# Experts' down product as six matmuls on high and low halves, with the down weights split tile by tile on ScalarE and GpSimd

## The reference

```python
x = hidden_states.reshape(-1, hidden_dim)              # 4096 x 512, after a layernorm
routing_weights = sigmoid(x @ Wg.T)                    # 8 experts
_, top_k_index = lax.top_k(routing_weights + bias, 2)  # 2 experts a token
expert_w = ...                                         # their weights, over their sum
h1 = einsum('th,efh->tef', x, W1)
h3 = einsum('th,efh->tef', x, W3)
g = silu(h1) * h3 * expert_w[:, :, None]
out = einsum('tef,ehf->th', g, W2)                     # the down product; FFN = 256
```

## Time and profile before

| | us |
|---|---|
| median of 3 runs | 2990.41 (2989.74 to 2998.49) |
| the profiled execution's own time | 2994.48 |
| its span | 2993.0 |
| busy in the span: TensorE / VectorE / ScalarE / GpSimd | 2650.0 / 1905.4 / 1376.0 / 1000.0 |
| granted TensorE clock, mean | 0.957 |

### The profile page before, as it was taken

One profiled execution on the slowest core, in us unless ns is written; L12 is line 12 of the kernel. 1 busy time (PEld: TensorE's weight loads), 2 busy tenths in 40 slices (PEclk: granted clock), 3 DMA queues, 4 the chain that ended last, 5 costly groups with the idle time before them and its releaser, 6 DMA issues. The chain is left out here.

```text
span 2993.0 us, 49729 instructions
## 1 busy us (share of the span) xinstructions
PE 2650.0 (89%) x15042; PEld 1820.6 (61%) x15043; DVE 1905.4 (64%) x3930; ACT 1376.0 (46%) x2757; POOL 1000.0 (33%) x1210
## 2 busy tenths in 40 slices
PE   7999999999999999997688888888888734589998
PEld 6888888888888888885233333333333222356665
DVE  6555566556556665555788888888888557344443
ACT  4333444444334443333376667677766632222222
POOL 2111122211112221113355556555654447122222
PEclk9999999999999999998799999999999867799999
DMA  3110011122101111102767677767666456545554
GB/s 113 43 42 15 28 42 42 42 68 87 43 3 40 42 42 42 42 29 56 131 118 127 129 137 133 135 126 139 127 127 120 83 187 242 170 78 99 99 99 83
DMA packets 141060, 265.55 MB, mean 89 GB/s; under 512 B 39216, under 2 KB 42160, under 8 KB 139456
## 3 DMA queue, kind: packets, MB, share of 16 engines
q1 hardware_dynamic: 114064, 200.83, 29.2%
q0 software_dynamic: 23856, 58.61, 10.1%
q10 hardware_dynamic: 3072, 5.25, 0.5%
HBM read 139.43 MB, written 64.90 MB: 68 GB/s over the span
## 5 line engine op out<-in xcount | busy, mean ns | idle before, releaser
L1420 DVE TENSOR_REDUCE b_negmax<-b_ps_s 128x2 f32<-128x1024 f32 x512 | 615.8, 1221 | 113.6 <-PE b_ps_s L1563 108.3
L1292 ACT ACTIVATE b_probs<-b_ps_s 128x1024 f32<-128x1024 f32 x512 | 517.2, 1022 | 262.4 <-PE b_ps_s L1574 261.1
L260 POOL TENSOR_SCALAR probs<-probs,rinv 128x256 f32<-128x256 f32 x256 | 242.6, 947 | 1099.6 <-DVE rinv L412 1099.6
L294 ACT ACTIVATE probs<-ps_s,negmax 128x128 f32<-128x128 f32 x256 | 94.2, 368 | 481.7 <-DVE negmax L405 481.7
L1574 PEld LDWEIGHTS b_ps_s<-b_stack 56*128 56x128 f32 x1024 | 96.8, 186 | 336.7 <-issue 182.3
L1574 PE MATMUL b_ps_s<-b_stack 56*128 56x512 f32 x1024 | 252.2, 491 | 55.2 <-DVE b_negmax L1420 38.5
L1563 PE MATMUL b_ps_s<-b_stack 54*128 54x512 f32 x1024 | 228.0, 442 | 80.5 <-ACT b_probs L1292 50.2
L1585 PE MATMUL b_ps_o<-b_probs,b_v_stack 128*32 128x512 f32 x2048 | 281.3, 622 | 5.7 <-ACT b_probs L1292 5.7
L516 PE MATMUL ps_proj<-xT_h,wq_h 128*128 128x512 f32 x512 | 215.6, 421 | 0.0
L2231 POOL DMA_INDIRECT out<-e_y,e_place_int x71 | 110.6, 1558 | 313.3 <-DMA out<-e_y,e_place_int 171.2
L516 PE MATMUL ps_proj<-xT_h,wq_l 128*128 128x512 f32 x512 | 201.3, 393 | 0.0
(11 more groups left out here) (315 smaller groups left out, 6793.0 us busy)
## 6 DMA issues: line engine op xcount, KB each, us to landing
b_stack<-b_split SPq DMA_DIRECT2D x240, 128.0 KB
e_row<-rows_by_expert SPq DMA_DIRECT2D x71, 258.0 KB
x_in<-in_x SPq DMA_DIRECT2D x16, 1024.0 KB, 7.6
b_out_tiles<-row_sum_inverses SPq DMA_DIRECT2D x64, 256.0 KB
x<-acc SPq DMA_DIRECT2D x15, 1024.0 KB, 5.0
b_stack<-b_late SPq DMA_DIRECT2D x96, 128.0 KB
acc<-in_x SPq DMA_DIRECT2D x8, 1024.0 KB, 6.0
acc<-x SPq DMA_DIRECT2D x8, 1024.0 KB, 5.9
```

The source lines that it names most:

```text
L260: nc.gpsimd.tensor_scalar(probs[:, s, P:3 * P], probs[:, s, P:3 * P], rinv[:, s, 1:2], None, ALU.mult).then_inc(probs_done, 1)
L294: nc.scalar.activation(probs[:, s, 0:P], ps_s[s][:, 0:P], ACT.Exp, bias=negmax[:, s, 0:1], accum_out=rowsum[:, s, 0:1])
L1292: nc.scalar.activation(probs[:, k % 2, p, :, :], ps[:], ACT.Exp, scale=0.25).then_inc(e_done, 1)
L1420: nc.vector.tensor_reduce(negmax[:, k, p, :], ps[:], AX.X, ALU.max, negate=True).then_inc(m_reduced, 1)
```

## The change

The down product takes the form of the other one: `g` transposed and the down weights are each split into a high and a low part in fp32r, and three matmuls are made for each of the two blocks of depth, six in all, in place of two in fp32.

- TensorE: `down` waits for `gT_low` and `w2_low` and makes 6 matmuls of 128x512.
- ScalarE: `gT_copy` writes the high part of `gT` and also waits for `y_filled`; after `high(u+1)` a new step, `down_weights_high(u)`, waits, loads the expert's number and copies that expert's `w2` (128x1024) to `w2_of[i][0]`.
- VectorE: a new step `g_low(u-1)` stands at the head of the tile, ahead of `low(u+1)`.
- GpSimd: a new step `down_weights_low(u)` stands at the head of the tile, ahead of the add of tile u-1: it waits for `w2_high`, loads the expert's number and subtracts, 128x1024, two inputs in SBUF.

```diff
-        gT = sb("gT", [P, FT, P])
+        gT = [sb(f"gT_{s}", [P, FT, P], F32R) for s in "hl"]
+        w2_of = [[sb(f"w2_{s}{i}", [P, FT, H], F32R) for s in "hl"] for i in range(2)]
...
+        def expert_at(eng, u):
+            at = tile_expert_int[0:1, u:u + 1] if isinstance(u, int) else tile_expert_int[0:1, bass.ds(u, 1)]
+            return bass.ds(eng.value_load(at, min_val=0, max_val=E - 1), 1)
...
+                def down_weights_low(u, i):
+                    pool.wait_ge(w2_high, u + 1)
+                    if not isinstance(u, int) or u >= 2:
+                        pool.wait_ge(y_filled, u - 1)
+                    nc.gpsimd.tensor_tensor(w2_of[i][1][:], w2[:, expert_at(pool, u), :, :].rearrange("p o f h -> p (o f) h"),
+                                      w2_of[i][0][:].bitcast(F32), ALU.subtract).then_inc(w2_low, 1)
+
                 def tile(u, t, i):
+                    down_weights_low(u, i)
                     if not isinstance(u, int) or u:
                         add_to_tokens(u - 1, 1 - i)
...
                 def gT_copy(u):
                     act.wait_ge(g_transposed, u + 1)
-                    nc.scalar.activation(gT[:], ps_g[:], ACT.Copy).then_inc(gT_done, 1)
+                    if not isinstance(u, int) or u:
+                        act.wait_ge(y_filled, u)
+                    nc.scalar.activation(gT[0][:], ps_g[:], ACT.Copy).then_inc(gT_high, 1)
+
+                def down_weights_high(u, i):
+                    if isinstance(u, int) and u == 0:
+                        act.wait_ge(w2_loaded, 16)
+                    if not isinstance(u, int) or u >= 2:
+                        act.wait_ge(y_filled, u - 1)
+                        wait_alone(act, w2_low, u - 1, (gT_high, 1))
+                    nc.scalar.activation(w2_of[i][0][:], w2[:, expert_at(act, u), :, :].rearrange("p o f h -> p (o f) h"),
+                                         ACT.Copy).then_inc(w2_high, 1)
...
+                def g_low(u):
+                    dve.wait_ge(gT_high, u + 1)
+                    nc.vector.tensor_tensor(gT[1][:], ps_g[:], gT[0][:].bitcast(F32), ALU.subtract).then_inc(gT_low, 1)
...
                 def tile(u, t, i):
+                    if not isinstance(u, int) or u:
+                        g_low(u - 1)
                     if not isinstance(u, int) or u < TILES - 1:
                         low(u + 1, 1 - i)
...
-                def down(u, i, e):
-                    pe.wait_ge(gT_done, u + 1)
-                    if isinstance(u, int) and u == 0:
-                        pe.wait_ge(w2_loaded, 16)
+                def down(u, i):
+                    pe.wait_ge(gT_low, u + 1)
+                    pe.wait_ge(w2_low, u + 1)
                     if not isinstance(u, int) or u >= 2:
                         pe.wait_ge(y_copied, u)
+                    n = 0
                     for f in range(FT):
-                        w = w2[:, e, f, :] if isinstance(e, int) else w2[:, bass.ds(e, 1), f, :].rearrange("p o h -> p (o h)")
-                        ins = nc.tensor.matmul(ps_y[i][:], gT[:, f, :], w, start=(f == 0), stop=(f == FT - 1))
+                        for a, c in PASSES:
+                            ins = nc.tensor.matmul(ps_y[i][:], gT[a][:, f, :], w2_of[i][c][:, f, :],
+                                                   start=(n == 0), stop=(n == 3 * FT - 1))
+                            n += 1
                     ins.then_inc(y_filled, 1)
```

More of the change, by code:

```diff
@@ L2201, in run_experts @@
         g_transposed = sem("g_transposed")
-        gT_done = sem("gT_done")
+        gT_high = sem("gT_high")
+        gT_low = sem("gT_low")
+        w2_high = sem("w2_high")
+        w2_low = sem("w2_low")
         w13_loaded = [sem(f"w13_loaded{n}") for n in range(2)]
@@ L2259, in tile @@
                         high(u + 1, 1 - i)
+                    down_weights_high(u, i)
                     act.wait_ge(h_filled, u + 1)
@@ L2334, in _ @@
                 in_steps(dve, TILES, tile, first=E, last=3)
+                g_low(TILES - 1)
                 y_copy(TILES - 1, (TILES - 1) // 2, (TILES - 1) % 2)
@@ L2376, in tile @@
                     e = expert_of(i)
-                    e_before = None if first else expert_of(1 - i)
                     if isinstance(u, int) and SPLIT_FIRST <= u < E:
@@ L2389, in tile @@
                                 if not first:
-                                    down(u - 1, 1 - i, e_before)
+                                    down(u - 1, 1 - i)
                                 if not last:
@@ L2402, in _ @@
                 g_transposes(TILES - 1)
-                down(TILES - 1, (TILES - 1) % 2, expert_of((TILES - 1) % 2))
+                down(TILES - 1, (TILES - 1) % 2)
 def decoder_layer(nc, x, context, mask, mask_cols, a_wq, a_wkv, a_wd, x_wq, x_bq, x_wk, x_bk, x_wv, x_bv,
```

## The result

Four runs of the changed kernel gave a median of 3038.05 us (3031.24 to 3046.59), the kernel before beside them 2990.07 us: a ratio of 1.0159, interval 1.0140 to 1.0178, which is slower by 47.5 us. I had forecast 3012 us and a range up to 3037, so the result lies outside the range. The sign and the main mechanism came as forecast; the size is more than twice the +21 us of the sum.

A forecast was written before the change was run, and what follows sets the result against it. TensorE sets the pace, the row-load loop through `meta` nearly as tight. Steady tiles +14.4, splitting tiles +3.8, first tile +1, landings +2, end 0: together +21 us on 2990.4, 3012 us; 8-in-10 range 2982 to 3037.

The forecast's parts named there:

- `meta` held to the subtraction's end: VectorE: `e_is_best`, sharing a port lock with GpSimd's subtraction, ends at +5.45 and `meta` at +5.97, 1.2 us later than now.
- the row loop as the bound: Late `meta`, 1.03 us on SyncE, then a row load of 3.95 us, needed two tiles later: a tile of 5.48 us.
- `down` behind `g_low` as the second: TensorE: `g_low` queues behind `meta` and ends near +6.5, `down` is due at +6.06: a tile of 5.15 us at least.
- the first tiles' copy: First tile: ScalarE's 1.05 us copy of the down weights stands ahead of the first gate, +1 us.
- clean gain: Rival, chance 0.15: `meta` isn't held up because the subtraction starts after it; 2971 to 2981 us.
- even: Rival, chance 0.14: `meta` is late but rows land in some 3.3 us, `down` sets 5.15 to 5.25 us; 2990 to 2998 us.
- the row load in full company: Rival, chance 0.21: loads still take 4.7 us, or ScalarE's register load isn't hidden; 3026 to 3041 us.
- when GpSimd subtracts: GpSimd: after ScalarE's copy ends at +2.28 and a 0.71 us register load, the subtraction runs from +3.05 to +5.41.
- one mean load in one bound: Row load taken as 3.95 us, from 2.9 to 4.7, giving a tile of 5.48 us that covers the wait at `down`.
- the landings at +2: GpSimd: adds that wait for landings also hold back the subtraction behind them, about eight times 0 to 0.7 us, +2 us.
- the splitting tiles: Six tiles at the start: `e_is_best` ends at 2613.7 instead of 2613.08, delaying `c_w_l` by 0.6 us each, +3.8 us.
- the end: Last adds: the landings of adds set the time as now, 0 us.

The follow-up runs named there:

- e6_meta_before: The kernel before with VectorE's meta(u+1) moved ahead of low(u+1) and the old down product kept: ratio to before 0.9971.
- e5_combo: The changed kernel with meta(u+1) ahead of low(u+1), register loads ahead of the waits, and GpSimd's subtraction behind the add in tiles 0 to 3: 0.9938 of before.
- e3_loads: The changed kernel with the register loads of the expert's number on ScalarE and GpSimd put ahead of their waits: ratio to before 1.0076.
- e8_noadds: The changed kernel with each add to out replaced by a DMA of 128 numbers within SBUF: one execution, 5.39 us a steady tile.
- e12_combo8: The changed kernel with meta(u+1) ahead of low(u+1), register loads ahead of waits, and the subtraction behind the add in tiles 0 to 7: 0.9950 of before.
- e9_swap_first8: The changed kernel with GpSimd's subtraction behind the add, meant for the first eight tiles but effective in tiles 0 to 3 only: ratio to before 1.0121.
- e2_meta: The changed kernel with VectorE's meta(u+1) moved from behind g(u) to between g_low(u-1) and low(u+1): ratio to before 0.9970.
- e7_lock_meta: The kernel before plus an unread GpSimd subtraction ahead of each add, with meta(u+1) ahead of low(u+1): ratio to before 1.0058.
- e10_memset: The kernel before plus a GpSimd fill of a 128x2048 spare buffer ahead of each add: one execution, 5.21 us a steady tile.
- e1_nosplit: The changed kernel with the down weights split for tiles 0 and 1 only, later tiles reusing those: ratio to before 0.9973.

## Where the prediction was right, and which steps failed

**Right.** The sign, and the way of the loss. The down product: 1.71 to 1.40 us said, 0.31 less; with the rows out of the way the median tile takes 5.22 us with the old product (e6_meta_before) and 4.88 with the new (e5_combo), 0.34 less. `meta` held to the subtraction's end; the row loop as the bound; `down` behind `g_low` as the second; no wait for the split weights; the clock at 1.00 in the steady stretch; the first tiles' copy, +1 us (12.2 instead of 11.1 us for the first two). The sign to look for was not quite met: I had said `e_is_best` of 1.5 us and more in nearly every tile, and it is so in 28 of 58. In others `e_not_best` or `e_best_weight` is the one that is held; one of the three takes 1.5 us or more in 42 tiles.

The rivals "clean gain" and "even" are out. The number fell into "the row load in full company", 3026 to 3041 us, though its condition held for part of the tiles only: tiles 10 to 25 had loads of 4.3 us and more, but the mean load was 3.71 us, not 4.7, and ScalarE's register load was hidden.

**The step that failed, first: "when GpSimd subtracts".** I had the subtraction at +3.05 and its end at +5.41; medians are +3.64 and +6.02. The copy starts at +1.47 and not at +1.23 (I had put nothing between the end of `high` and the copy; it is 0.2 us), and from the copy's end to the subtraction it is 1.11 us instead of 0.77. By e3_loads the register load is 0.86 of that, where I had 0.71, and 0.25 remain without it, where I had 0.06. The row load is issued at +7.50 on average instead of +7.00. Half of that a tile, 60 times, is +15 us.

**Second: one mean load in one bound.** The load's mean, 3.71 us, was even below my 3.95, worth -7 us. But I put the mean into the rows' bound and let the other bound, which I had at 5.15 us, lie below it throughout. The loads come in groups of tiles. In tiles 10 to 25 every one took 4.3 to 5.3 us, and a tile 6.02 us on average. In tiles 26 to 33 every one took 2.6 to 3.4 us, and a tile still 5.45: the rows land early, but `down` waits for `g_low`, so these tiles don't win back what the others lost. One of them:

```profile
2790.74 2.36 DVE L2327 TENSOR_TENSOR e_not_best<-e_row,c_tile_expert 128x1 f32<-128x1 f32 x1
...
2793.47 0.42 DVE L2319 TENSOR_TENSOR e_gT_l<-e_ps_g,e_gT_h 128x256 fp32r<-128x256 f32 x1
```

```profile
2791.79 0.60 PE L2378 MATMUL e_ps_x<-c_ident,e_row 128*128 128x128 f32 x4
...
2793.94 0.50 PE L2395 MATMUL e_ps_y<-e_w_h,e_gT_h 128*128 128x512 f32 x1 [0.85 <-DVE e_gT_l L2319]
```

`down` starts at +2.15 instead of +1.13, although the rows had landed 0.5 us before their transposes. On average rows lay there for 0.28 us; half of that, 60 times, is +8 us. 15 - 7 + 8 = 16 us, which takes the 14.4 of the sum to +30.5. (Exact to a tenth is luck: I also had the old tile at 5.24 us and it is 5.27, -2 us, and the landings at +2.) That both bounds act is shown by e8_noadds (5.39 us with the rows never late).

**Third: the splitting tiles, +0.6 us each.** They cost +1.6. The mechanism was named, but the row was the wrong one: in the earlier trace rows `e_is_best` began at 2612.93, +5.1 in its tile; that tile's transposes began with TensorE still at 1.2 GHz (granted clock 0.50 from 2607.80 to 2609.90, behind the wait of 3.87 us that ended at 2603.80). In the five other tiles it began at +4.1 to +4.6, so there the subtraction's end, +5.4 by my own sum, puts it off by 0.7 to 1.2 us and not by 0.6. In the changed kernel `c_w_l` starts 1.3 us later on average (+6.3 instead of +5.0), and TensorE waits for it 32.7 us in all instead of 23.2:

```profile
PE e_ps_h L2393 <- DVE c_w_l L2328: 23.2, 6, 3.9
```

```profile
PE e_ps_h L2429 <- DVE c_w_l L2362: 32.7, 6, 5.7
```

That is 9.5 of the +10.6 us. A term that I had put at nothing is here too, the clock. Its mean over these tiles fell from 0.78 to 0.74 (the last three numbers of each line are clock, DMA share, GB/s), and TensorE was busy for as long as before, although its own work had become shorter:

```profile
2560.00:2641.00 81.00, 52.45 (x161) 35.66 (x162) 30.80 (x73) 22.10 (x29) 10.68 (x8) 0.78 0.41 104
```

```profile
2560.00:2652.00 92.00, 52.28 (x174) 39.08 (x175) 44.32 (x80) 29.55 (x36) 27.12 (x15) 0.74 0.37 92
```

In e12_combo8, with the same six matmuls and waits of 19.7 us for `c_w_l`, TensorE was busy 48.3 us in the first eight tiles, at a mean of 0.81. Longer waits and a lower mean clock come together in these runs, and none prices one apart from the other. e9_swap_first8 shows the size of both together, some 2 us a tile.

**Fourth: the end, 0.** It took 3.1 us more, in two parts. The two tiles from tile 68 to 70 took 12.2 instead of 10.5 us, with a wait for rows (a load of 5.0 us ahead of tile 70) and one for `g_low`: +1.7, the same cause as above. From the last transposes to the end it is 26.5 instead of 25.2 us, +1.4. This part isn't late `meta`: it is there with `meta` early (26.4 us in e2_meta, 26.1 in e5_combo, 27.1 in e7_lock_meta) and with the fill in place of the subtraction (26.6 in e10_memset), and not where GpSimd has nothing new there (25.0 in e1_nosplit, 24.7 in e6_meta_before). So it goes with GpSimd's work ahead of the last adds, which the prediction had put at nothing.

One thing stays open: why a row load issued 1.3 us behind an add takes 3.0 us in some tiles and 4.4 in others. In the changed kernel neighbouring tiles keep to one or the other, in e1_nosplit and in the kernel before the two mostly take turns, and e9_swap_first8, with the same code in these tiles, has them in another order.

## What to carry to other kernels

Before work is moved to GpSimd, look for the VectorE instructions with two inputs in SBUF that will run beside it, however small, and ask what is queued behind them; here 0.15 us on 128x1 numbers carried the row loads, and moving it into an idle gap turned +1.6% into -0.3%. Take such a sum from medians over many tiles and not from one row, and where now one bound holds and now another, sum the larger of the two tile by tile and not the bound of the mean. On GpSimd a register load is better put ahead of the wait than behind it: 0.86 us a tile here.

## What the hardware showed beside that

A GpSimd fill of 128x2048 (1.81 us) leaves a VectorE instruction with two SBUF inputs at its 0.15 us; a copy with one SBUF input (1.89 us) holds it until the copy's end (1.68 us); two GpSimd subtractions one behind the other held it through both (5.27 us, seen once, in e12_combo8). A row load of 258 KB takes 2.64 us (median) when issued 0.25 us ahead of an add (e10_memset), and 2.6 to 4.7 us when issued 1.3 us behind one (the changed kernel). A register load behind a wait on GpSimd costs 0.86 us of the 1.11 from the wait's end to the subtraction; ahead of the wait 0.25 are left (e3_loads).
